# Adjacency masks as packed bytes, written by GpSimd and turned four at a time as float32

## The chip, the core and the metric

The kernel runs on one core of a Trainium2 chip. TensorE multiplies and transposes into PSUM, VectorE, ScalarE and GpSimd compute element by element (GpSimd on SBUF alone), and the queue of SyncE (SP) issues all the DMA transfers. The metric is the device time of one execution in microseconds; smaller is better.

## The reference

Two graph attention layers over 8192 nodes with 128 features and one adjacency matrix of 8192 x 8192 int32 (about 0.4% ones). Each layer normalises x, takes the ReLU, multiplies by W, and sums over the neighbours:

```
h  = relu(layernorm(x));  Wh = h @ W
e  = leaky_relu((Wh @ a_src)[:, None] + (Wh @ a_dst)[None, :], 0.2)
att = softmax(where(adj > 0, e, very negative), axis=1)
layer 0: att = where(att >= 1e-4, att, 0) * (number of neighbours)
         x = x + elu(Wh + att @ Wh)
layer 1: x = x + att @ Wh
```

The number of neighbours counts adj > 0 in each row. Layer 0 leaves out small weights, and layer 1 doesn't.

## The kernel before

A short preparation makes h, its row and column terms and their exponentials for each layer. Then a path follows that the data choose; with this input it is the fast one, `fast_path_0` for layer 0 and `fast_path_1` for layer 1. The weight of edge (i, j) is written as max(r_i, rho_j) times the mask times D_j, where D_j is multiplied into h once (`fold`, eight parts). So no exponential is taken per edge.

Layer 0 works on 16 groups of four row tiles (512 rows), with a loop over the groups 2 to 13 (`groups_of`). Each group passes over the columns in four chunks of 2048, that is 16 column tiles a chunk and 64 a group. The work per chunk:

- SP loads four pieces of int32, one for each row tile k, into `adj_in[k]` (L861). There are four such buffers in all. A piece for the next chunk is loaded when its mask has been made (semaphore `masked`).
- VectorE makes a bf16 mask of each piece (`mark`, L995) in `edges`, two buffers of four tiles.
- ScalarE sums each mask along its rows for the number of neighbours (`count`, L908).
- TensorE turns the masks: for a pair of column tiles eight bf16 transposes (L951) into one of four PSUM banks (`RING`).
- VectorE forms the weights of one column tile for 512 rows from that bank (`form`, L1002): max of `r_row` and `rho_col`, times the mask, into float32 `wTs`.
- ScalarE copies the bank as bytes into `edge_out` (L919), and SP stores a chunk of it to `edgesT` (L884), which layer 1 reads in place of the adjacency matrix.
- TensorE multiplies the weights by h, one float32 product for each row tile (L968); each is two instructions. All 64 column tiles add up in PSUM.

The order on TensorE is: turn pair p + 2, sum pair p. On VectorE: form a pair, and in the first four of each chunk's eight pairs one mask of the next chunk behind it. On ScalarE: copy a pair, and in the same places count. After pair 5 and pair 11 of a group VectorE finishes the group before (`finish`, `finish_elu`), with an ELU by ScalarE between. Before the store of the finished rows SP waits for it (`out_ready`), with the next chunk's loads behind it in its queue.

Layer 1 has eight groups of eight row tiles. Its two loads a chunk bring the masks of two groups of layer 0, 1 MB each, in pieces of 8192 bytes a partition (L1128); VectorE forms 1024 weights at a time (L1178), and TensorE makes eight products (L1162). GpSimd does nothing but three constants at the start.

Of the kernel before, what the change touches and what calls it, by code (L numbers as in the profile page):

```python
# [13 lines left out]
ALU = mybir.AluOpType  # L14
# [4 lines left out]
U8 = mybir.dt.uint8  # L19
I32 = mybir.dt.int32  # L20
# [32 lines left out]
PAIRS = T // 2  # L53
RING = 4
CP = PAIRS // NC
# [9 lines left out]
def kernel_program(nc, x, adj, W0, a0, W1, a1, out):  # L65
# [15 lines left out]
    with ctx:  # L81
# [90 lines left out]
        def prepare(layer, x_in, W_in, a_in):  # L172
# [68 lines left out]
            with nc.Block() as block:  # L241
                @block.sync
                def _(sp):
# [211 lines left out]
        def general_path(layer, x_in, x_to):  # L455
# [305 lines left out]
            return sync_rows, scalar_rows, tensor_rows, vector_rows  # L761

# [31 lines left out]
        def load_r(sp, r_loaded, i):  # L794

            c = slice(0, G0 * P) if i == 0 else slice(G0 * P, G1 * P) if i == 1 else slice(G1 * P, N)
            sp.dma_start(r_row[:, c], r_mid[:, c].partition_broadcast(P)).then_inc(r_loaded[i], 16)  # L797
# [10 lines left out]
        def fast_path_0(x_in, x_to):  # L808
# [22 lines left out]
            edges = [part(at + i * GI * CB // 2, GI * CB // 2).bitcast(BF16).rearrange("p (t c) -> p t c", t=G0)  # L831
                     for i in range(2)]
            at += GI * CB
            wTs = [part(at + i * 2 * GI, 2 * GI) for i in range(RING)]
            at += RING * 2 * GI
            edge_out = [part(at + i * CB * GI // 4, CB * GI // 4).bitcast(U8) for i in range(2)]
            at += CB * GI // 2
# [9 lines left out]
            edge_ps = [bank(i).bitcast(BF16) for i in range(RING)]  # L847

            x_view = x_in.rearrange("(g t p) f -> g p t f", p=P, t=G0)
            h_view = h_mid.rearrange("(g t p) f -> g p t f", p=P, t=G0)  # L850
            out_view = x_to.rearrange("(g t p) f -> g p t f", p=P, t=G0)

            def sync_rows(sp):
                def group(it, g):
                    for c in range(NC):
                        for k in range(G0):
# [4 lines left out]
                            sp.dma_start(adj_in[k], adj_view[it * (2 * G0) + (g * G0 + k), :, c, :])\  # L861
# [7 lines left out]
                        if c == 2:  # L869
                            if g >= 1:  # L870
                                wait_in(sp, out_ready, it, 1, g)
                                sp.dma_start(out_view[it * 2 + (g - 1)], xo.rearrange("p (t f) -> p t f", t=G0))\
                                    .then_inc(stored, 16)
                            sp.dma_start(xr.rearrange("p (t f) -> p t f", t=G0), x_view[it * 2 + g])\
                                .then_inc(res_loaded, 16)
                            sp.dma_start(hr.rearrange("p (t f) -> p t f", t=G0), h_view[it * 2 + g])\
                                .then_inc(res_loaded, 16)

                def store_edges(it, g, c):
                    if c < 0:  # L880
                        g, c = g - 1, c + NC

                    wait_in(sp, copied, it, PAIRS, g * PAIRS + (c + 1) * CP)
                    sp.dma_start(edgesT[it * (2 * NC) + (g * NC + c)], edge_out[c % 2]).then_inc(edges_stored[c % 2], 16)  # L884
# [6 lines left out]
                sp.dma_start(out_view[NG - 1], xo.rearrange("p (t f) -> p t f", t=G0)).then_inc(stored, 16)  # L891
                sp.wait_ge(stored, 16 * NG)
                for i in range(2):
                    sp.wait_ge(edges_stored[i], 16 * NG * NC // 2)

            def scalar_rows(act):
                def count(it, g, c, k):
# [10 lines left out]
                    nc.scalar.activation(copies, edges[c % 2][:, k, :], ACT.Identity,  # L908
                                         accum_out=cnt[g % 2][:, k, c:c + 1]).then_inc(counted, 1)

                def group(it, g):
                    for p in range(PAIRS):
                        c, q = p // CP, p % CP
                        m = g * PAIRS + p

                        wait_in(act, formed, it, 2 * PAIRS, 2 * (m + 1))
                        if q == 0 and g * NC + c >= 2:
                            act.wait_ge(edges_stored[c % 2], it * (NC * 16) + (g * NC + c) // 2 * 16)
                        nc.scalar.activation(edge_out[c % 2][:, q * 2 * GI:(q + 1) * 2 * GI], edge_ps[m % RING],  # L919
                                             ACT.Identity).then_inc(copied, 1)  # L920
# [17 lines left out]
            def tensor_rows(pe):  # L938
                def turn_pair(it, g, p):
                    if p >= PAIRS:  # L940
# [352 lines left out]
```

## Time and profile before

| | |
|---|---|
| Runs | 2295.46, 2295.52, 2297.7 us, median 2295.52 |
| Profiled execution, its span | 2295.8 us |
| Layer 0's path, layer 1's path in it | 1196.0 us, 928.6 us |
| TensorE, VectorE, ScalarE busy | 2161.5, 1843.8, 1047.8 us |
| Granted TensorE clock, mean | 0.978 of full speed |
| DMA | 448.32 MB, mean 195 GB/s |

The page was taken in one execution whose span, 2295.8 us, is its own time. The busy time of an engine is the time in which at least one of its instructions is under way. The mean duration of a matmul is longer than its pace, since matmuls overlap; the pace is busy time over count, or the distance of starts in the timeline.

### The profile page before, as it was taken

The page shows a single profiled execution, that of the slowest core. Times are in us where ns is not written, and L with a number is a line of the kernel's source. Part 1 is how long each engine was busy: PE and PEld are TensorE (multiplying, and loading weights), DVE is VectorE, ACT ScalarE, POOL GpSimd, SP SyncE. Part 2 cuts the span into 40 slices and gives each one's busy share as a digit, 9 for nine tenths or more (in the row PEclk, how much of TensorE's full clock was granted, in tenths as well). Part 3 has the DMA queues.
Part 4 walks back from the last instruction along what each step waited for, and adds up shares of the span by engine and source line. Part 5 has one row for each costly group of instructions (what it writes and reads, how often), then busy time and mean ns, then how long its engine had stood idle before and what let it go on. Part 6 is the DMA issues. An engine that isn't in the chain of part 4 may idle for free. (4 is left out here: it accounts for less than half of the span.)

```text
span 2295.8 us, 51629 instructions
## 1 busy us (share of the span) xinstructions
PE 2161.5 (94%) x20884; PEld 2145.0 (93%) x20884; DVE 1843.8 (80%) x2708; ACT 1047.8 (46%) x1206; POOL 1.0 (0%) x7
## 2 busy tenths in 40 slices
PE   5899999999999999999999369999999999999997
PEld 4799999999999999999999269999999999999997
DVE  6898888888888989888987657877777777777775
ACT  4788888888888878888887220000000000000000
POOL 0000000000000000000000000000000000000000
PEclk9899999999999999999999689999999999999999
DMA  6869776877777767876684332121212121212120
GB/s 221 353 264 356 293 274 237 347 303 272 269 312 304 295 249 304 330 281 268 277 350 150 92 150 83 73 93 74 93 74 92 75 92 74 92 74 92 74 93 11
DMA packets 112240, 448.32 MB, mean 195 GB/s; under 512 B 8320, under 2 KB 57984, under 8 KB 62592
## 3 DMA queue, kind: packets, MB, share of 16 engines
q1 hardware_dynamic: 112000, 444.89, 50.7%
q8 instruction: 179, 2.93, 0.5%
q14 instruction: 61, 0.50, 0.1%
HBM read 365.04 MB, written 79.82 MB: 194 GB/s over the span
## 5 line engine op out<-in xcount | busy, mean ns | idle before, releaser
L968 PE MATMUL psum<-h_all,arena 128*128 128x129 f32 x8192 | 1030.7, 279 | 1.2 <-DVE arena L1002 1.0
L968 PEld LDWEIGHTS psum<-h_all,arena 128*128 128x128 f32 x8192 | 959.0, 192 | 3.9 <-DVE arena L1002 2.3
L1162 PE MATMUL psum<-h_all,arena 128*128 128x129 f32 x8192 | 920.4, 276 | 23.6 <-DVE arena L1178 20.2
L1162 PEld LDWEIGHTS psum<-h_all,arena 128*128 128x128 f32 x8192 | 918.9, 192 | 25.2 <-issue 17.6
L1178 DVE SCALAR_TENSOR_TENSOR arena<-arena,rho_col 128x1024 f32<-128x1024 f32 (+1 forms) x512 | 653.8, 1284 | 234.8 <-PE psum L1162 225.6
L1002 DVE SCALAR_TENSOR_TENSOR arena<-arena,rho_col,psum 128x512 f32<-128x512 bf16 (+1 forms) x1024 | 710.5, 744 | 99.5 <-PE psum L951 94.8
L919 ACT ACTIVATE arena<-psum 128x1024 uint8<-128x1024 bf16 x512 | 510.5, 1021 | 154.8 <-DVE arena L1002 154.5
L908 ACT ACTIVATE arena<-arena 128x2048 bf16<-128x2048 bf16 x256 | 487.9, 1906 | 50.5 <-DVE arena L995 44.8
L995 DVE TENSOR_SCALAR arena<-arena 128x2048 bf16<-128x2048 int32 x256 | 313.1, 1224 | 38.1 <-DMA arena<-in_adj_dram 36.8
L951 PE MATMUL psum<-identb,arena 128*128 128x128 bf16 x4096 | 314.4, 220 | 22.4 <-DVE arena L995 9.8
L951 PEld LDWEIGHTS psum<-identb,arena 128*128 128x128 bf16 x4096 | 273.7, 99 | 29.9 <-DVE arena L995 9.9
L416 PE MATMUL psum<-ident,arena 128*128 128x128 f32 x128 | 23.5, 315 | 40.7 <-DVE arena L308 40.7
L416 PEld LDWEIGHTS psum<-ident,arena 128*128 128x128 f32 x128 | 17.8, 164 | 42.4 <-DVE arena L308 41.7
L908 ACT ACTIVATION_READ_ACCUMULATOR arena<-arena 128x1 f32 x256 | 49.2, 192 | 0.0
L424 PE MATMUL psum<-arena 128*128 128x131 f32 x256 | 39.1, 302 | 0.0
L424 PEld LDWEIGHTS psum<-arena 128*128 128x128 f32 x256 | 35.9, 215 | 0.6 <-ACT arena L396 0.4
L308 DVE TENSOR_SCALAR arena<-arena 128x128 f32<-128x128 f32 x128 | 33.5, 344 | 0.3
L284 DVE BATCH_NORM_STATS2 arena<-arena 128x6 f32<-128x128 f32 x128 | 25.5, 281 | 7.2 <-DMA arena<-in_x_dram 3.8
L396 ACT ACTIVATE arena<-psum 128x512 f32<-128x512 f32 x32 | 19.3, 602 | 17.0 <-PE psum L416 17.0
L385 ACT ACTIVATE h_all<-psum 128x512 f32<-128x512 f32 x32 | 19.1, 598 | 9.5 <-PE psum L424 7.8
L805 DVE TENSOR_TENSOR h_all<-h_all,D_col 128x1024 f32<-128x1024 f32 x16 | 19.5, 1221 | 0.0
L1032 DVE SCALAR_TENSOR_TENSOR arena<-psum,arena 128x128 f32<-128x128 f32 x64 | 18.0, 345 | 0.7 <-DVE arena L1028 0.2
(100 smaller groups left out, 178.3 us busy)
## 6 DMA issues: line engine op xcount, KB each, us to landing
arena<-in_adj_dram SPq DMA_DIRECT2D x256, 1024.0 KB, 8.3
edgesT<-arena SPq DMA_DIRECT2D x64, 1024.0 KB, 5.9
arena<-edgesT SPq DMA_DIRECT2D x64, 1024.0 KB, 6.6
arena<-r_mid SPq DMA_DIRECT2D x2, 3584.0 KB, 20.4
h_mid<-h_all SPq DMA_DIRECT2D x16, 256.0 KB, 2.3
arena<-in_x_dram SPq DMA_DIRECT2D x16, 256.0 KB, 3.1
arena<-h_mid SPq DMA_DIRECT2D x16, 256.0 KB, 3.5
x_mid<-arena SPq DMA_DIRECT2D x16, 256.0 KB, 2.5
```

The source lines that it names most:

```text
L284: last = nc.vector.bn_stats(st[:, t, :], x_all[:, t, :])
L308: last = nc.vector.tensor_scalar(hn[:, t, :], x_all[:, t, :], mean[:, t:t + 1], rstd[:, t:t + 1], ALU.subtract, ALU.mult)
L416: last = nc.tensor.transpose(hn_ps[q % 2][:, i * P:(i + 1) * P], hn[:, q * QT + i, :], ident[:])
L424: last = nc.tensor.matmul(h_ps[q % 2][:, i, :], hnT[q % 2][:, i * P:(i + 1) * P], W_ext, start=True, stop=True)
L908: nc.scalar.activation(copies, edges[c % 2][:, k, :], ACT.Identity, accum_out=cnt[g % 2][:, k, c:c + 1]).then_inc(counted, 1)
L919: nc.scalar.activation(edge_out[c % 2][:, q * 2 * GI:(q + 1) * 2 * GI], edge_ps[m % RING], ACT.Identity).then_inc(copied, 1)
L951: last = nc.tensor.transpose(edge_ps[m % RING][:, (b * G0 + k) * P:(b * G0 + k + 1) * P], edges[c % 2][:, k, (2 * q + b) * P:(2 * q + b + ...
L968: last = nc.tensor.matmul(acc_tile(g, G0, k), wTs[m % RING][:, b * GI + k * P:b * GI + (k + 1) * P], h_all[:, j, :], start=(j == 0 and k % ...
L995: nc.vector.tensor_scalar(edges[c % 2][:, k, :], adj_in[k], 0.0, None, ALU.is_gt).then_inc(masked, 1)
L1002: nc.vector.scalar_tensor_tensor(wTs[m % RING][:, b * GI:(b + 1) * GI], r_row[:, bass.ds(it * (2 * GI) + g * GI, GI)], rho_col[:, 2 * p + ...
L1162: last = nc.tensor.matmul(acc_tile(g, G1, k), wTs[m % RING][:, k * P:(k + 1) * P], h_all[:, j, :], start=(j == 0 and k % 2 == 0), stop=(j ...
L1178: nc.vector.scalar_tensor_tensor(wTs[m % RING].rearrange("p (h i) -> p h i", h=2), r_row[:, bass.ds(it * (2 * R1) + g * R1, R1)] .rearrang ...
```

## The change

Mask and turning, in layer 0. The masks of the four row tiles of a group are written as bytes into one buffer, `packs`, byte k of each float32 word for row tile k. GpSimd writes them (`pool_rows`), as min(adj, 1) and max with 0, with a step of four bytes. TensorE turns the words as float32, one transpose for four masks, in quads of four column tiles: a quad fills one bank. VectorE forms from every fourth byte of the bank. `wTs` has eight buffers of one column tile instead of four of two. ScalarE copies the bank as 1024 16-bit words, a quad at a time, and counts from the bytes. The order on TensorE is: turn quad q + 1, sum the four tiles of quad q.

Rows. Layer 1 wants its eight row tiles as bytes of words as well, so a group of layer 0 now takes every second row tile of eight: 0, 2, 4, 6 and then 1, 3, 5, 7. Loads, stores and `r_row` are addressed accordingly, and the first chunk's four loads, which the preparation issues, take these tiles too (`adj_view[2 * k, ...]`). In layer 1 the edge loads go into pieces of 512 bytes, and `form` reads its bytes with a step of four. The first part of `r_row` is 1024 wide in both layers, and its second part is loaded a little later in layer 1.

```diff
 RING = 4
-CP = PAIRS // NC
+WRING = 8
+QUAD = 4
+QUADS = T // QUAD
+CQ = QUADS // NC
...
-                            sp.dma_start(adj_in[k], adj_view[k, :, 0, :]).then_inc(adj_in_loaded[k], 16)
+                            sp.dma_start(adj_in[k], adj_view[2 * k, :, 0, :]).then_inc(adj_in_loaded[k], 16)
...
+            packs = [part(at + i * CH, CH) for i in range(2)]
+            pack_bytes = [p.bitcast(U8).rearrange("p (n k) -> p n k", k=G0) for p in packs]
...
+            edge_bytes = [bank(i).bitcast(U8).rearrange("p (b i k) -> p b k i", b=QUAD, k=G0) for i in range(RING)]
+            edge_words = [bank(i).bitcast(U16) for i in range(RING)]
...
+            rows_view = adj.rearrange("(a k h p) (c n) -> a h k p c n", k=G0, h=2, p=P, n=CH)
...
-                            sp.dma_start(adj_in[k], adj_view[it * (2 * G0) + (g * G0 + k), :, c, :])\
+                            sp.dma_start(adj_in[k], rows_view[it + g // 2, g % 2, k, :, c, :])\
...
+            def pool_rows(pool):
+                def group(it, g):
+                    for c in range(NC):
+                        u = g * NC + c
+                        for k in range(G0):
+                            pool.wait_ge(adj_in_loaded[k], it * (2 * NC * 16) + (u + 1) * 16)
+                            if k == 0:
+                                wait_in(pool, turned, it, QUADS, (u - 1) * CQ)
+                            wait_in(pool, counted, it, NC * G0, (u - 2) * G0 + k + 1)
+                            nc.gpsimd.tensor_scalar(pack_bytes[c % 2][:, :, k], adj_in[k], 1.0, 0.0,
+                                                    ALU.min, ALU.max).then_inc(masked, 1)
...
-                    for p in range(PAIRS):
-                        c, q = p // CP, p % CP
-                        m = g * PAIRS + p
-
-                        wait_in(act, formed, it, 2 * PAIRS, 2 * (m + 1))
+                    for q in range(QUADS):
+                        c, r = q // CQ, q % CQ
+                        m = g * QUADS + q
+
+                        wait_in(act, formed, it, T, QUAD * (m + 1))
...
-                        if q < G0:
-                            count(it, g, c + 1, q)
-                        if p == 9 and g >= 1:
+                        count(it, g, c + 1, r)
+                        if q == 4 and g >= 1:
...
-                    wait_in(pe, copied, it, PAIRS, m - RING + 1)
-                    for b in range(2):
-                        for k in range(G0):
-                            last = nc.tensor.transpose(edge_ps[m % RING][:, (b * G0 + k) * P:(b * G0 + k + 1) * P],
-                                                       edges[c % 2][:, k, (2 * q + b) * P:(2 * q + b + 1) * P],
-                                                       identb[:])
+                    wait_in(pe, copied, it, QUADS, m - RING + 1)
+                    for b in range(QUAD):
+                        last = nc.tensor.transpose(edge_ps[m % RING][:, b * P:(b + 1) * P],
+                                                   packs[c % 2][:, (QUAD * r + b) * P:(QUAD * r + b + 1) * P], ident[:])
...
-                    nc.vector.tensor_scalar(edges[c % 2][:, k, :], adj_in[k], 0.0, None, ALU.is_gt).then_inc(masked, 1)
...
+                def form(it, g, j):
+                    m = g * T + j
+                    if j % QUAD == 0:
+                        wait_in(dve, turned, it, QUADS, m // QUAD + 1)
+                    wait_in(dve, summed, it, T, m - WRING + 1)
+                    r_four = r_row[:, bass.ds(it * (2 * GI) + g // 2 * (2 * GI), 2 * GI)]\
+                        .rearrange("p (k h i) -> p k h i", k=G0, h=2)[:, :, g % 2, :]
+                    nc.vector.scalar_tensor_tensor(wTs[m % WRING].rearrange("p (k i) -> p k i", k=G0), r_four,
+                                                   rho_col[:, j:j + 1], edge_bytes[m // QUAD % RING][:, j % QUAD],
+                                                   ALU.max, ALU.mult).then_inc(formed, 1)
...
-                        if p == 5 and g >= 1:
+                        if j == 9 and g >= 1:
                             finish(it, g - 1)
-                        if p == 11 and g >= 1:
+                        if j == 22 and g >= 1:
                             finish_elu(it, g - 1)
...
-                            sp.dma_start(edges[c % 2][:, h].rearrange("p b i -> p (b i)"),
-                                         edgesT[it * (4 * NC) + ((2 * g + h) * NC + c)]).then_inc(edges_loaded[c % 2], 16)
+                            sp.dma_start(edges[c % 2][:, :, h, :],
+                                         edgesT[it * (4 * NC) + ((2 * g + h) * NC + c)]
+                                         .rearrange("p (b w) -> p b w", b=CB)).then_inc(edges_loaded[c % 2], 16)
```

On TensorE at the start of layer 0, before (L951 turns with `identb`, L968 sums):

```order
L1234 COMPARE_AND_BRANCH
L951 MATMUL psum<-identb,arena 128x128 x24
L968 MATMUL psum<-h_all,arena 128x129 x8
L951 MATMUL psum<-identb,arena 128x128 x8
L968 MATMUL psum<-h_all,arena 128x129 x8
```

and after (L970 turns with `ident`, L984 sums):

```order
L1237 COMPARE_AND_BRANCH
L970 MATMUL psum<-ident,arena 128x128 x8
L984 MATMUL psum<-h_all,arena 128x129 x16
L970 MATMUL psum<-ident,arena 128x128 x4
L984 MATMUL psum<-h_all,arena 128x129 x16
```

Eight transposes for every eight products have become four for every sixteen.

On VectorE, where group 1 finishes group 0, before (L1002 forms, L995 makes a mask, L1017 to L1032 finish):

```order
L995 TENSOR_SCALAR arena<-arena 128x2048
L1002 SCALAR_TENSOR_TENSOR arena<-arena,rho_col,psum 128x512 x4
L1017 TENSOR_REDUCE arena<-arena 128x4
L1019 COPY arena<-psum 128x1 x4
L1022 TENSOR_SCALAR arena<-r_col,low_exp 128x4
L1024 SCALAR_TENSOR_TENSOR at_risk<-arena 128x4
L1025 TENSOR_SCALAR arena<-arena 128x4
L1026 RECIPROCAL arena<-arena 128x4
L1028 TENSOR_TENSOR arena<-arena 128x4
L1032 SCALAR_TENSOR_TENSOR arena<-psum,arena 128x128 x4
L1002 SCALAR_TENSOR_TENSOR arena<-arena,rho_col,psum 128x512 x6
L995 TENSOR_SCALAR arena<-arena 128x2048
```

and after (L1006 forms, L1019 to L1034 finish, L1041 to L1045 are the second part):

```order
L1006 SCALAR_TENSOR_TENSOR arena<-arena,rho_col,psum 128x512 x25
L1019 TENSOR_REDUCE arena<-arena 128x4
L1021 COPY arena<-psum 128x1 x4
L1024 TENSOR_SCALAR arena<-r_col,low_exp 128x4
L1026 SCALAR_TENSOR_TENSOR at_risk<-arena 128x4
L1027 TENSOR_SCALAR arena<-arena 128x4
L1028 RECIPROCAL arena<-arena 128x4
L1030 TENSOR_TENSOR arena<-arena 128x4
L1034 SCALAR_TENSOR_TENSOR arena<-psum,arena 128x128 x4
L1006 SCALAR_TENSOR_TENSOR arena<-arena,rho_col,psum 128x512 x13
L1041 TENSOR_SCALAR arena<-arena 128x512
L1042 SCALAR_TENSOR_TENSOR arena<-arena 128x512
```

The masks are gone from VectorE, and the finishing stands nearly where it stood: after 10 and 23 column tiles of the next group instead of 12 and 24.

On GpSimd, which had no row in layer 0, there is now the branch and one row:

```order
L1236 TENSOR_LOAD path
L1236 ISA x2
L1237 COMPARE_AND_BRANCH
L911 ISA
L911 TENSOR_SCALAR arena<-arena 128x2048 x256
```

All 256 masks stand behind one another, each with its waits for the loaded piece, for the turning of the chunk two before, and for its count.

## Rows read from the trace of the kernel before

**Rows 1.** Page: the span, and each engine's busy time, share and instructions.

```profile
span 2295.8 us, 51629 instructions
...
PE 2161.5 (94%) x20884; PEld 2145.0 (93%) x20884; DVE 1843.8 (80%) x2708; ACT 1047.8 (46%) x1206; POOL 1.0 (0%) x7
```

**Rows 2.** Page: the chain that ended last, shares of the span by line.

```profile
PE psum L1162 38%; DVE arena L1201 1%; DVE arena L1178 1%; DVE arena L1208 1%; DMA arena<-edgesT 0%; DVE arena L1192 0%; DVE arena L1196 0%; DVE arena L1195 0%; DVE arena L1194 0%; SPq L797 0%; SPq L1233 0%; SPq L1128 0%; DVEq L1245 0%; DVEq L776 0%; DVEq L1197 0%
```

**Rows 3.** Windows of both layers' paths: busy us (instructions), clock, DMA share, GB/s.

```profile
68.00:1264.00 1196.00, 1181.91 (x12288) 1171.74 (x12288) 1046.31 (x1540) 993.10 (x1052) 0.00 (x0) 0.99 0.75 292
1351.40:2280.00 928.60, 918.64 (x8178) 917.33 (x8179) 697.15 (x707) 0.00 (x0) 0.00 (x0) 1.00 0.23 82
```

**Rows 4.** Waits: engine and line, what it waited for, us in total, times, longest.

```profile
DVE arena L1002 <- PE psum L951: 94.8, 131, 2.1
...
DVE arena L995 <- DMA arena<-in_adj_dram: 36.8, 25, 2.7
```

**Rows 5.** Page, groups: count, busy us, mean ns, idle before and its releaser.

```profile
L1162 PE MATMUL psum<-h_all,arena 128*128 128x129 f32 x8192 | 920.4, 276 | 23.6 <-DVE arena L1178 20.2
...
L1178 DVE SCALAR_TENSOR_TENSOR arena<-arena,rho_col 128x1024 f32<-128x1024 f32 (+1 forms) x512 | 653.8, 1284 | 234.8 <-PE psum L1162 225.6
L1002 DVE SCALAR_TENSOR_TENSOR arena<-arena,rho_col,psum 128x512 f32<-128x512 bf16 (+1 forms) x1024 | 710.5, 744 | 99.5 <-PE psum L951 94.8
L919 ACT ACTIVATE arena<-psum 128x1024 uint8<-128x1024 bf16 x512 | 510.5, 1021 | 154.8 <-DVE arena L1002 154.5
L908 ACT ACTIVATE arena<-arena 128x2048 bf16<-128x2048 bf16 x256 | 487.9, 1906 | 50.5 <-DVE arena L995 44.8
L995 DVE TENSOR_SCALAR arena<-arena 128x2048 bf16<-128x2048 int32 x256 | 313.1, 1224 | 38.1 <-DMA arena<-in_adj_dram 36.8
```

**Rows 6.** Timeline of layer 0, settled: start us, us, engine, line, operation.

```profile
501.52 0.61 PE L951 MATMUL psum<-identb,arena 128*128 128x128 bf16 x8
...
501.97 2.00 PE L968 MATMUL psum<-h_all,arena 128*128 128x129 f32 x16
...
503.81 0.61 PE L951 MATMUL psum<-identb,arena 128*128 128x128 bf16 x8
```

**Rows 7.** Timeline of the preparation of layer 1, TensorE.

```profile
1310.03 0.60 PE L416 MATMUL psum<-ident,arena 128*128 128x128 f32 x4
...
1310.47 1.06 PE L424 MATMUL psum<-arena 128*128 128x131 f32 x8
```

**Rows 8.** Timeline of GpSimd, all that it does before the change.

```profile
0.25 0.10 POOL L1280 MEMSET const-float32-0.0<- 128x1 f32 x1 [0.25 <-issue]
...
0.74 0.20 POOL L159 MEMSET ident<- 128x128 f32 x1 [0.29 <-POOLq L1280]
...
1.53 0.29 POOL L164 CAST identb<-ident 128x128 bf16<-128x128 f32 x1
```

**Rows 9.** Timeline of layer 0's first instructions.

```profile
62.10 0.23 DVE L803 COPY h_all<-D_col 128x64 f32<-128x64 f32 x1 [3.27 <-issue]
...
68.03 2.74 PE L951 MATMUL psum<-identb,arena 128*128 128x128 bf16 x24 [9.76 <-DVE arena L995]
```

**Rows 10.** Timeline of layer 0's last row group being finished by VectorE.

```profile
1263.86 0.17 DVE L1017 TENSOR_REDUCE arena<-arena 128x4 f32<-128x16 f32 x1 [4.01 <-PE psum L968]
...
1265.34 1.13 DVE L1032 SCALAR_TENSOR_TENSOR arena<-psum,arena 128x128 f32<-128x128 f32 x4
...
1267.82 0.43 DVE L1039 TENSOR_SCALAR arena<-arena 128x512 f32<-128x512 f32 x1 [1.36 <-ACT arena L931]
...
1269.01 0.69 DVE L1043 TENSOR_TENSOR arena<-arena 128x512 f32<-128x512 f32 x1
```

**Rows 11.** Page, DMA issues: line, count, KB each, median us to landing.

```profile
arena<-in_adj_dram SPq DMA_DIRECT2D x256, 1024.0 KB, 8.3
```

**Rows 12.** Windows: loads in pieces of 512 bytes, then loads in long pieces.

```profile
1282.00:1298.00 16.00, 1.06 (x3) 0.68 (x3) 9.55 (x53) 0.43 (x2) 0.00 (x0) 0.50 0.94 259
1344.00:1352.00 8.00, 0.57 (x3) 0.61 (x4) 2.01 (x2) 0.00 (x0) 0.00 (x0) 0.50 1.01 425
```

More of the change, by code:

```diff
@@ L19 @@
 U8 = mybir.dt.uint8
+U16 = mybir.dt.uint16
 I32 = mybir.dt.int32
@@ L829, in fast_path_0 @@
             at = 2 * N
[L831 to L837, printed above, removed]
+            packs = [part(at + i * CH, CH) for i in range(2)]
+            pack_bytes = [p.bitcast(U8).rearrange("p (n k) -> p n k", k=G0) for p in packs]
+            at += 2 * CH
+            wTs = [part(at + i * GI, GI) for i in range(WRING)]
+            at += WRING * GI
+            edge_out = [part(at + i * CB * P, CB * P).bitcast(U16) for i in range(2)]
+            at += 2 * CB * P
             copies = part(at, CH // 2).bitcast(BF16)
@@ L894, in sync_rows, with pool_rows @@
                     sp.wait_ge(edges_stored[i], 16 * NG * NC // 2)
+            def pool_rows(pool):
+                def group(it, g):
[8 more added lines that the diff above has]
+                                                    ALU.min, ALU.max).then_inc(masked, 1)
+                for g in range(NG):
+                    group(0, g)
             def scalar_rows(act):
@@ L959, in sum_pair @@
                         wait_in(pe, acc_read, it, 1, g - 1)
-                    for b in range(2):
-                        j = 2 * p + b
-                        if g == 0 and j % (T // FOLDS) == 0:
-                            pe.wait_ge(h_folded, j // (T // FOLDS) + 1)
-                        wait_in(pe, formed, it, 2 * PAIRS, m * 2 + b + 1)
-                        for k in range(G0):
-                            last = nc.tensor.matmul(acc_tile(g, G0, k),
-                                                    wTs[m % RING][:, b * GI + k * P:b * GI + (k + 1) * P],
-                                                    h_all[:, j, :], start=(j == 0 and k % 2 == 0), stop=(j == T - 1),
-                                                    skip_group_check=True)
+                    if g == 0 and j % (T // FOLDS) == 0:
+                        pe.wait_ge(h_folded, j // (T // FOLDS) + 1)
@@ L972, in sum_pair @@
+                    wait_in(pe, formed, it, T, m + 1)
+                    for k in range(G0):
+                        last = nc.tensor.matmul(acc_tile(g, G0, k), wTs[m % WRING][:, k * P:(k + 1) * P],
+                                                h_all[:, j, :], start=(j == 0 and k % 2 == 0), stop=(j == T - 1),
+                                                skip_group_check=True)
                     last.then_inc(summed, 1)
                 def group(it, g):
-                    for p in range(PAIRS):
-                        turn_pair(it, g, p + 2)
-                        sum_pair(it, g, p)
```

123 lines of the change are left out of this document (57 added, 66 removed).

## The prediction

> **What bounds the kernel now.** I read the page's first part, then the chain, then a table of stretches, then the waits, and last the timeline of a settled stretch. TensorE is busy 94% of the span and VectorE 80%, while GpSimd does nothing [rows 1]. The chain that ended last is TensorE's products of layer 1 and ends there after 38% of the span [rows 2]; it does not reach back into layer 0, so the table of stretches has to say what binds there. It gives layer 0's path 1196.0 us (68.0 to 1264.0) and layer 1's 928.6 us. In the first, TensorE is busy 1181.9 us at a granted clock of 0.99, VectorE 1046.3 us (87%), ScalarE 993.1 us (83%); in the second TensorE is busy 918.6 of 928.6 us [rows 3]. VectorE's two largest waits in layer 0 are for turned tiles, 94.8 us, and for the adjacency loads, 36.8 us [rows 4]. So TensorE binds both paths, and VectorE is close behind it in the first.
>
> The settled timeline gives TensorE's cycle: the eight bf16 transposes of a pair start at 501.52, its eight float32 products (16 instructions) at 501.97, the next transposes at 503.81 [rows 6]. That is 0.45 us of turning and 1.84 us of summing, 2.29 us for a pair of column tiles, and 512 pairs make 1172 us. The other 24 us of the 1196 are cold or uneven stretches at the start and losses between.
>
> **TensorE's work after the change.** The products stay: 16 for each four column tiles. The 16 bf16 transposes of these four tiles become 4 float32 ones, because one float32 element holds four mask bytes. The price of a float32 transpose stands in the preparation: four of them start at 1310.03 and the next product at 1310.47 [rows 7], 0.11 us each, 0.44 us for four. A product costs 920.4 / 4096 = 0.225 us in layer 1, where nothing interrupts them [rows 5], and 1.84 / 8 = 0.230 us between transposes [rows 6]. The change from turning to summing thus costs about 0.04 us each time, and the longer runs pay it half as often: 16 x 0.225 + 0.04 = 3.64 us. A quad of column tiles then costs 3.64 + 0.44 = 4.08 us where two pairs cost 4.58. 256 quads save 256 x 0.50 = 128 us. With products at 0.230 it is 118 us, with 0.225 and no change-over cost 138 us.
>
> **VectorE.** It loses the 256 masks, 313.1 us [rows 5]. It keeps 1024 forming instructions, now reading one byte of each 4-byte word of PSUM and a row vector in four pieces. No row shows a byte read from PSUM. From below the price is today's 710.5 / 1024 = 0.69 us [rows 5], since 512 elements are still 512 elements. The row of layer 1 with two operands from SBUF, one of them bytes, has 1024 elements in 1.284 us, 1.25 ns each or 0.64 us for 512, so byte operands cost nothing visible there. From above I take one such instruction of twice the elements, 1.28 us. I choose 0.70: the words touched are those that a float32 read would touch. Four formings are then 2.8 us beside TensorE's 4.08, and VectorE is hidden with 1.2 us to spare per quad. At 1.28 us it would be 5.1 us and the new bound. Layer 1's forming reads its bytes with the same step; it takes 1.28 us beside 8 x 0.225 = 1.80 us of TensorE, and it would have to become 0.5 us slower to matter. I cost it at nothing.
>
> **ScalarE.** 256 copies instead of 512 (1.02 us each [rows 5], the same 1024 elements) and the same 256 counts (1.91 us). Per quad 2.9 us and a short accumulator read beside 4.08, hidden; the copy's relief of 255 us is worth nothing in time. The count now stands behind a GpSimd mask, and behind the count stands the next copy, and TensorE turns into a bank only when the copy of four quads earlier is done. A late mask stops the whole ring by that way.
>
> **GpSimd, the open cost.** 256 masks of 2048 int32 elements to bytes four apart. It needs one mask per quad, so it stays hidden up to 4.08 us and costs nothing in the balance up to 4.58 us, today's time of two pairs. The trace has no such instruction. Its nearest rows are a memset of one element, 0.10 us, a memset of 128, 0.20 us, and a cast of 128, 0.29 us [rows 8]. With 0.10 us fixed, the cast costs 1.5 ns an element and a mask 3.1 us; the memset's slope gives 1.7 us; the cast without any fixed part gives 16 x 0.29 = 4.6 us. I take 3.1 us, because a fixed part is plainly there and a mask reads and writes as the cast does. Beyond these ends the row doesn't exclude more, since the input is an integer and there are two operations.
>
> The Trainium skill (GPSIMD Engine Reference, section 3.1) gives 1.03 cycles an element at 1.2 GHz for a body of up to two operations and about 1.8 for a tight loop otherwise; as an estimate that makes 1.8 to 3.1 us a mask, on the same side of 4.08. No run here shows that yet.
>
> **Start.** VectorE's first instruction in layer 0 is at 62.10 and TensorE's first transpose at 68.03 [rows 9], after four masks of 1.22 us. Now four masks by GpSimd stand there: 62.1 + 4 x 3.1 + 0.1 = 74.6, 6.6 us later, say 7. Masks of 1.7 us would make it 1 us, of 4.6 us 13 us. Against that, part of the 24 us of losses came from VectorE, which formed and masked at once; I give back 4 of them, with 0 and 15 as the ends.
>
> **Loads and queues.** SP keeps its order. The four adjacency buffers are refilled after each mask, each load lands 8.3 us after its issue [rows 11], and a chunk lasts 4 x 4.08 = 16.3 us; a buffer freed after its own 3.1 us is full again at 11.4 us. Traffic in layer 0 rises from 292 GB/s to 292 x 1196 / 1075 = 325, at a DMA share of 0.75 x 1.11 = 0.83 [rows 3], while 425 GB/s at full share is seen with long pieces [rows 12]. SP still stops in every group before the output store, and the four loads behind it come in one burst; GpSimd's buffers absorb that, as each chunk is masked about one chunk ahead of its turning. Layer 1's edge loads now land in pieces of 512 bytes. Loads of that kind moved 259 GB/s against 425 [rows 12]. In the settled part 2 MB are wanted per 29 us, so it is hidden. At the start 2 MB stand in front of the first forming: 8.1 us instead of 4.9 at most, of which I count 2 us, as issue and latency overlap.
>
> **VectorE against GpSimd.** VectorE finishes a row group in 1263.86 to 1266.47, 2.6 us, and again in 1.9 us [rows 10]. These instructions stand at the third and the sixth quad of the next group. TensorE has 1.4 us and 2.2 us in hand there with the new ring of eight. No row shows the two engines at work together. I count 8 us for the whole path (16 groups and seven foldings of h), with 0 below; the upper end is the second rival's.
>
> The Trainium skill (SBUF — State Buffer, section "Who interferes with whom") speaks against this change: a Vector instruction with two SBUF inputs, or in a two-port mode, and a GpSimd instruction that reads SBUF exclude each other for the whole instruction. No run here shows it yet.
>
> **Sum.** 2295.8 - 128 + 7 - 4 + 8 + 2 = 2181 us. The profiled span, 2295.8, lies 0.3 us above the median of the runs, 2295.52, so nothing is converted. Forecast: 2181 us, 5% faster, with its own range 2158 to 2200.
>
> **Rivals.** First, GpSimd becomes the bound, the case that ends slower. Masks then follow one another without a gap: 62.1 + 256 T and the last chunk's 16 us; against today's end of the path at 1264 this breaks even at T = 4.6 us. At 5.5 us it costs 256 x (5.5 - 4.6) = 230 us: 2525 us, and more if TensorE's clock falls in the gaps. For it: an integer input, a strided byte output and two operations in no row. Against it: the rows reach only 4.6 us at the worst. Between 4.08 and 4.6 us it ends between 2190 and 2296.
>
> Second, the change is made but VectorE and GpSimd hold each other up. Foldings and finishes that meet a mask wait up to 3.1 us. The finish and the second part have together five or six instructions with two SBUF operands or fast copies. If two waits of 3.1 us fall in each half, 2 x 3.1 - 1.4 = 4.8 and 2 x 3.1 - 2.2 = 4.0 us stop TensorE, 8.8 us x 15 groups = 132 us: 2305. If only one wait in each half does, 2.6 us x 15 = 39 us: 2215. For it: masks fill 12.4 of 16.3 us. Against it: they begin when a chunk's last quad has been turned, so that the third quad, 12.2 us on, finds them done. The one at the sixth quad meets the last mask alone.
>
> Third, the loads can't follow. If layer 0 stays at 292 GB/s nothing is gained: 2296. With the 36.8 us of waits [rows 4] at their present size but now on the path: 2215. For it is SP's burst; against it 425 GB/s in rows 12.
>
> Fourth, byte reads from PSUM cost 1.28 us: 256 x (5.1 - 4.58) = 133 us more, 2430 us.
>
> **Chances.** The forecast 0.66; masks over 4.6 us 0.13; masks of 4.08 to 4.6 us 0.05; the two engines against each other 0.10 (of it 0.02 slower than before); the loads 0.04; byte reads 0.02. The range 2155 to 2300 leaves out the first rival's slow part, the fourth and the tail below, 0.19 together. A change of 0.2% is what a measurement of this kernel can tell from none. Faster: 0.66 + 0.04 + 0.07 + 0.02 = 0.79; within 0.2%: 0.04; slower: 0.17.
>
> **What would show it.** In the profile after, GpSimd has 256 instructions, and from start to start within a chunk they lie 3 us apart; 4.1 or more means the first rival. TensorE's transposes in layer 0 number 1024, four in 0.44 us, and quads follow at 4.08 us. VectorE's forming stays at 0.69 to 0.75 us; waits of VectorE inside the finish would speak for the second rival, GpSimd waiting for the adjacency loads with TensorE waiting for GpSimd for the third. Layer 1's products take 920 us as before. The forecast is wrong if the median is over 2200 us or if TensorE waits for masks beyond the first chunk.

## The result and the profile after

The changed kernel takes 2183.59 us (median of 3, 2180.18 to 2185.07) against 2295.52 us, a ratio of 0.9505 [0.9489, 0.9522]. The forecast was 2181 us. The sum came out; some of its terms did not, and the experiments say which.

The page of the kernel after, its first part, the chain that ended last and the groups that answer to [rows 1, 2, 5]:

```profile
span 2181.8 us, 44712 instructions
PE 2023.8 (93%) x17812; PEld 2015.4 (92%) x17812; DVE 1563.2 (72%) x2452; ACT 808.1 (37%) x950; POOL 639.2 (29%) x263
...
PE 40%; DVE 2%; DMA 1%; issue 1%; SPq 0%; DVEq 0%
...
L984 PE MATMUL psum<-h_all,arena 128*128 128x129 f32 x8192 | 969.0, 277 | 0.2 <-DVE arena L1006 0.2
...
L1162 PE MATMUL psum<-h_all,arena 128*128 128x129 f32 x8192 | 920.8, 276 | 28.2 <-DVE arena L1178 22.4
...
L1006 DVE SCALAR_TENSOR_TENSOR arena<-arena,rho_col,psum 128x512 f32<-128x512 uint8 (+1 forms) x1024 | 693.9, 742 | 274.0 <-PE psum L970 256.0
L1178 DVE SCALAR_TENSOR_TENSOR arena<-arena,rho_col 128x1024 f32<-128x1024 f32 (+1 forms) x512 | 653.7, 1284 | 239.8 <-PE psum L1162 228.4
L911 POOL TENSOR_SCALAR arena<-arena 128x2048 uint8<-128x2048 int32 x256 | 638.2, 2528 | 480.9 <-DMA arena<-in_adj_dram 282.1
...
L970 PE MATMUL psum<-ident,arena 128*128 128x128 f32 x1024 | 156.9, 277 | 42.0 <-issue 27.6
```

TensorE still binds both layers. VectorE fell from 80% to 72% and waits 256 us for turned tiles, GpSimd has one mask per quad at 2.5 us, and layer 1's two large groups are what they were. The waits of TensorE after:

```profile
PE psum L970 <- issue: 27.6, 5, 5.7
PE psum L1162 <- DVE arena L1178: 22.4, 7, 15.9
PE psum L970 <- POOL arena L911: 14.4, 1, 14.4
...
PE psum L1162 <- issue: 5.8, 1, 5.8
```

TensorE waits for a mask once, at the start, and never for a copy or a forming in the settled part. What stands out is "issue" (idle time for which the profile shows nothing that the engine waits for), five times 5.5 us, of which the prediction spoke nowhere. The settled stretch, TensorE alone (start, duration), answers to [rows 6]:

```profile
501.58 0.60 PE L970 MATMUL psum<-ident,arena 128*128 128x128 f32 x4
502.02 3.74 PE L984 MATMUL psum<-h_all,arena 128*128 128x129 f32 x32
505.60 0.60 PE L970 MATMUL psum<-ident,arena 128*128 128x128 f32 x4
506.03 3.74 PE L984 MATMUL psum<-h_all,arena 128*128 128x129 f32 x32
509.61 0.60 PE L970 MATMUL psum<-ident,arena 128*128 128x128 f32 x4
```

From transposes to transposes it is 4.01 us: 0.43 for four float32 transposes, 3.58 for 16 products. And this is the same engine where the loop over row groups jumps back, the first of five such places:

```profile
328.46 0.60 PE L970 MATMUL psum<-ident,arena 128*128 128x128 f32 x4
328.90 3.74 PE L984 MATMUL psum<-h_all,arena 128*128 128x129 f32 x32
338.24 1.11 PE L970 MATMUL psum<-ident,arena 128*128 128x128 f32 x4 [5.61 <-issue]
339.14 5.77 PE L984 MATMUL psum<-h_all,arena 128*128 128x129 f32 x32
344.75 0.60 PE L970 MATMUL psum<-ident,arena 128*128 128x128 f32 x4
```

The engine stands still for 5.6 us with nothing in the profile that it waits for, and the next quad takes 6.5 us instead of 4.01, with transposes at 1.11 us instead of 0.60: from 338 to 344 us the granted clock is 0.55, near the lower of its two levels (1.2 of 2.4 GHz), after it was 1.00 until the stop. This jump costs 9.78 + 6.51 - 2 x 4.01 = 8.3 us, the other four 8.0 to 8.1 us each, and the five 40.5 us. In the trace of before the same five jumps have gaps of 2.4 to 2.7 us, three of them with a slower pair behind, 18.0 us together. They are hard to see there, since the wait rows put three of them down to ScalarE's copy:

```profile
PE psum L951 <- ACT arena L919: 7.8, 3, 2.7
PE psum L951 <- issue: 4.9, 2, 2.4
```

The 114.0 us between the two spans divide as follows. The quads' pace: 256 x (4.58 - 4.01) = 146 us less. Stops and slow stretches in layer 0, which is all that the quads' pace leaves over: 44.8 us instead of 23.3, 21.5 more; at the five jumps alone 40.5 instead of 18.0. TensorE's start in layer 0: 72.39 instead of 68.03, 4.4 more. Between the layers: 90.9 instead of 87.6 us, 3.3 more, since VectorE's first forming of layer 1 waits 11.4 us for the edge loads instead of 9.2. Layer 1: 2.8 more, mostly its own one jump (5.8 us after, 3.5 before).

### The profile page after: what moved, and what is told of

It is laid out like the page before. It is cut to its first block and busy times, and to the rows that moved or that the text cites. A ratio compares the mean times of both kernels' runs of the same rounds, so it can differ in the third digit from the quotient of the medians.

```text
span 2181.8 us, 44712 instructions
## 1 busy us (share of the span) xinstructions
PE 2023.8 (93%) x17812; PEld 2015.4 (92%) x17812; DVE 1563.2 (72%) x2452; ACT 808.1 (37%) x950; POOL 639.2 (29%) x263
## 5 line engine op out<-in xcount | busy, mean ns | idle before, releaser
L984 PE MATMUL psum<-h_all,arena 128*128 128x129 f32 x8192 | 969.0, 277 | 0.2 <-DVE arena L1006 0.2
L984 PEld LDWEIGHTS psum<-h_all,arena 128*128 128x128 f32 x8192 | 947.1, 194 | 1.1 <-issue 0.5
L1162 PE MATMUL psum<-h_all,arena 128*128 128x129 f32 x8192 | 920.8, 276 | 28.2 <-DVE arena L1178 22.4
L1006 DVE SCALAR_TENSOR_TENSOR arena<-arena,rho_col,psum 128x512 f32<-128x512 uint8 (+1 forms) x1024 | 693.9, 742 | 274.0 <-PE psum L970 256.0
L911 POOL TENSOR_SCALAR arena<-arena 128x2048 uint8<-128x2048 int32 x256 | 638.2, 2528 | 480.9 <-DMA arena<-in_adj_dram 282.1
L929 ACT ACTIVATE arena<-arena 128x2048 bf16<-128x2048 uint8 x256 | 487.9, 1906 | 37.8 <-POOL arena L911 37.8
L940 ACT ACTIVATE arena<-psum 128x1024 uint16<-128x1024 uint16 x256 | 261.4, 1021 | 287.1 <-DVE arena L1006 286.4
L970 PE MATMUL psum<-ident,arena 128*128 128x128 f32 x1024 | 156.9, 277 | 42.0 <-issue 27.6
L970 PEld LDWEIGHTS psum<-ident,arena 128*128 128x128 f32 x1024 | 122.4, 143 | 43.2 <-issue 28.5
L419 PE MATMUL psum<-ident,arena 128*128 128x128 f32 x128 | 24.0, 320 | 41.4 <-DVE arena L311 41.4
L419 PEld LDWEIGHTS psum<-ident,arena 128*128 128x128 f32 x128 | 18.3, 167 | 43.1 <-DVE arena L311 42.4
L287 DVE BATCH_NORM_STATS2 arena<-arena 128x6 f32<-128x128 f32 x128 | 25.5, 277 | 6.9 <-DMA arena<-in_x_dram 3.6
L801 DVE TENSOR_TENSOR h_all<-h_all,D_col 128x1024 f32<-128x1024 f32 x16 | 26.4, 1651 | 0.0
L1041 DVE TENSOR_SCALAR arena<-arena 128x512 f32<-128x512 f32 x16 | 6.8, 427 | 21.9 <-ACT arena L951 21.9
```

What stands on the lines that cost most here:

```text
L419: last = nc.tensor.transpose(hn_ps[q % 2][:, i * P:(i + 1) * P], hn[:, q * QT + i, :], ident[:])
L801: nc.vector.tensor_tensor(h_all[:, c, 0:F], h_all[:, c, 0:F], D[:, c].to_broadcast([P, T // FOLDS, F]), ALU.mult).then_inc(h_folded, 1)
L911: nc.gpsimd.tensor_scalar(pack_bytes[c % 2][:, :, k], adj_in[k], 1.0, 0.0, ALU.min, ALU.max).then_inc(masked, 1)
L929: nc.scalar.activation(copies, pack_bytes[c % 2][:, :, k], ACT.Identity, accum_out=cnt[g % 2][:, k, c:c + 1]).then_inc(counted, 1)
L940: nc.scalar.activation(edge_out[c % 2][:, r * 2 * GI:(r + 1) * 2 * GI], edge_words[m % RING], ACT.Identity).then_inc(copied, 1)
L970: last = nc.tensor.transpose(edge_ps[m % RING][:, b * P:(b + 1) * P], packs[c % 2][:, (QUAD * r + b) * P:(QUAD * r + b + 1) * P], ident[:])
```

## The experiments

**1. TensorE's loop of layer 0 written out.** In the changed kernel:

```
-                groups_of(pe, NG, group)
+                for g in range(NG):
+                    group(0, g)
```

> The changed kernel with TensorE's loop over the groups of layer 0 written out (no jump back; every other engine keeps its loop). Theory A (TensorE waits for its own instructions after each of the five jumps, behind the bulk loads in the DMA engines): the gaps of 5.4 to 5.7 us and the slow quad behind each go, 8.3 us x 5 = 41 us, so 2183.6 - 41 = about 2142 us. Rival B (TensorE stands there because data or other engines are late): the gaps stay, 2179 to 2188 us.

Measured: 2142.08 us, 0.9328 [0.9313, 0.9344] of before, 41.5 us less than the change alone. The stops and the slow quads behind them are gone; from 72.4 to 1090 us TensorE is busy 1017.43 of 1017.6 us. Theory A holds to the microsecond.

**2. The same edit in the kernel before.**

> The kernel before, with TensorE's loop over row groups of layer 0 written out (no jump), the other engines as they are. Theory A (TensorE's own stop at the jump of its loop costs time in both kernels, 23.3 us over five jumps before and 44.8 after): 2295.8 - 20 = 2276 us, 2270 to 2282; written out, the change is then worth 2276 - 2142 = 134 us instead of 112. Theory B (before, TensorE's stops at the jump are covered by VectorE, which is late there anyway): no difference, 2296 us.

Measured: 2281.53 us, 0.9942 [0.9925, 0.9958], 14 us less. Theory A, at the small end. The gaps put down to ScalarE's copy are gone as well, so they too belonged to the jump. The expectation's 23.3 us were not all at the jumps: these had cost 18.0 us, and TensorE's part of layer 0 is 16.0 us shorter in the profile (1179.8 instead of 1195.8 us). So with TensorE's jumps of layer 0 gone on both sides the change is worth 2281.5 - 2142.1 = 139.4 us; 28 of these (41.5 - 14.0) were given away at five jumps.

**3. Every quad's transposes twice.** `for b in [*range(QUAD), *range(QUAD)]` in place of `for b in range(QUAD)`.

> The changed kernel, with the four float32 transposes of each quad issued twice (same data, same place). Theory A (TensorE binds layer 0, and a transpose costs its pace of 0.11 us in full): 256 x 0.44 = 113 us more, 2184 + 113 = 2296 us, 2288 to 2300. Theory B (part of a quad's 4.01 us is waiting for VectorE, ScalarE or GpSimd): clearly less, under 2270 us.

Measured: 2292.14 us, 0.9986 [0.9977, 0.9996], 108.5 us more or 0.424 us for four transposes, which is their pace in the timeline. Nothing in a quad's 4.01 us was waiting that could have hidden them: TensorE alone sets the pace of layer 0.

**4. Why the stop is long: lighter loads.**

```
+                            w = CH if g < 2 else CH // 4
-                            sp.dma_start(adj_in[k], rows_view[..., c, :])
+                            sp.dma_start(adj_in[k][:, :w], rows_view[..., c, :w])
```

> The changed kernel, but from the third row group of layer 0 on each adjacency load brings only the first quarter of its columns (this leaves out three quarters of the input; instructions, waits and loops are the same). Theory A (TensorE's stop at its loop jump is 5.4 to 5.7 us instead of 2.5 because the load traffic is full there, share 0.99): the stops go back to 2.7 us or less and the slow quad behind them goes, 5 x (8.3 - 4) = 20 us less, 2164 us, 2155 to 2170. Theory B (the longer stop belongs to the loop itself, whatever the loads do): the stops stay at 5.4 us and the time at 2184 us, 2178 to 2186.

Measured: 2173.74 us, 0.9472 [0.9456, 0.9488] of before, 10 us less than the change, between the two. The first jump there, TensorE alone:

```profile
329.31 3.74 PE L985 MATMUL psum<-h_all,arena 128*128 128x129 f32 x32
336.99 0.75 PE L971 MATMUL psum<-ident,arena 128*128 128x128 f32 x4 [3.94 <-issue]
337.53 5.32 PE L985 MATMUL psum<-h_all,arena 128*128 128x129 f32 x32
342.69 0.60 PE L971 MATMUL psum<-ident,arena 128*128 128x128 f32 x4
```

With the DMA share around the jump (326 to 346 us) down from 0.89 to 0.32 the stop is 3.9 us, not 2.7, and a slow quad still follows. So the light loads take 1.5 us off each stop, and with what hangs on it 2 us of the 8.1. That is no test without traffic, though. Inside the first stop itself the engines were still busy; the kernel before, the kernel after and the light loads (from and to, length, busy us of each engine, clock, DMA share, GB/s):

```profile
366.43:368.86 2.43, 0.00 (x1) 0.00 (x1) 2.02 (x3) 2.43 (x3) 0.00 (x0) 0.99 0.68 206
332.63:338.24 5.61, 0.01 (x2) 0.01 (x1) 1.74 (x3) 2.91 (x3) 3.92 (x2) 0.85 1.00 402
333.05:336.99 3.94, 0.00 (x1) 0.01 (x1) 0.00 (x0) 2.44 (x3) 2.33 (x1) 1.00 0.75 247
```

The traces show one thing more. In each stop a 16 KB transfer of the kind "instruction" starts on queue q8, and TensorE goes on 1.5 to 1.7 us after its start in all 40 jump stops of layer 0 in eight traces (before, after, and experiments 3 to 7). What differs is when it starts: within 0.2 us of the stop's beginning in the kernel before, 1.3 to 1.7 us later with the light loads, 2.9 to 3.1 us later in the changed kernel. So the whole difference between the stops lies ahead of that transfer. At TensorE's waits for masks in experiment 7 no such transfer stands at that distance. The profile does not say which engine it is for; that TensorE waits for it is read from this agreement, not tested.

**5. The other engines' jumps taken away.** SP, ScalarE and VectorE written out in layer 0, TensorE's loop left; then the same with the light loads.

> The changed kernel with the loops of SP, ScalarE and VectorE in layer 0 written out, and TensorE's left as a loop. Theory A (TensorE's stop is long because the other engines fetch their own loop bodies at the same time): its stops fall from 5.4 us to about 2.5 us and the quad behind them is less slow, 5 x 3 to 4 us, 2166 us, 2163 to 2170. Theory B (the stop is TensorE's own, whatever the others do): 2184 us, 2180 to 2186.

> The same with the light loads (from the third row group on each adjacency load brings only the first quarter of its columns, which leaves out three quarters of the input). With TensorE's loop alone and little traffic. Light loads by themselves gave 2174 us and stops of 4.0 us. Theory A (traffic and the other engines' fetches each add their part): stops of 2.5 us or less, 2160 us, 2155 to 2166. Theory B (only traffic adds): 2174 us, 2171 to 2176, stops of 4.0 us.

Measured: 2181.22 us, 0.9494 [0.9478, 0.9510], stops of 26.6 us in sum; and 2173.53 us, 0.9467 [0.9448, 0.9485], stops of 21.7 us. Theory B in both: the other engines' jumps cost TensorE nothing that can be told from noise. The stop belongs to TensorE's own jump, and lighter loads shorten it. Why 4.0 to 4.3 us remain with them, where it is 2.5 us before, stays open; since they left a share of 0.75 inside the stop, traffic may still be a part of it.

**6. GpSimd's masks in the kernel before.** The bf16 masks moved from VectorE to GpSimd, with everything else as before.

> The kernel before with its bf16 masks made by GpSimd (min with 1, max with 0) in place of VectorE, all else as before: the move to GpSimd alone. Theory A (TensorE binds with 2.29 us a pair, VectorE's relief is worth only the uneven stretches at the start): start 4 us later, 4 to 8 us won back, 2288 to 2300 us. Rival B (VectorE's 87% was what slowed layer 0): 60 us and more go, under 2240 us.

Measured: 2312.98 us, 1.0076 [1.0060, 1.0093], 13 us above theory A's range and far from rival B. The pair of column tiles still takes 2.29 us. Relieving VectorE by itself gains nothing and costs 17 us; the gain of the change is TensorE's cheaper turning. What theory A had not counted are the jumps: with the slower pairs behind them they cost 35.3 us instead of 18.0. Waits of TensorE and the group of masks there:

```profile
PE psum L966 <- issue: 26.5, 5, 5.5
...
PE psum L966 <- POOL arena L908: 12.3, 1, 12.3
```

```profile
L908 POOL TENSOR_SCALAR arena<-arena 128x2048 bf16<-128x2048 int32 x256 | 485.0, 1911 | 764.5 <-issue 446.9 <-DMA arena<-in_adj_dram 317.5
```

The longer stop is here too, with bf16 masks and bf16 transposes. So the packing is not needed for it. Nor is the move: the kernel of experiment 7, with packed masks by VectorE and GpSimd idle, has five such stops too, of 5.0 to 5.9 us. What the three kernels share is full load traffic inside the stop, a DMA share of 0.94 to 1.00 where it is 0.62 to 0.72 before; that this makes the stop long fits experiment 4 but was not tested by itself.

**7. The opposite: packed masks by VectorE.** GpSimd idle, a mask behind each quad's formings.

```
+                        if j % QUAD == QUAD - 1:
+                            mark(it, g, j // CB + 1, j // QUAD % G0)
```

> The changed kernel with the packed byte masks made by VectorE, one behind each quad of formings, and GpSimd idle: the packed turning alone. Theory A (a byte mask written with a step of four bytes costs VectorE the 1.22 us of the bf16 mask): VectorE has 1024 x 0.68 + 313 + 26 + 60 = about 1096 us of work in layer 0 where TensorE has 1071, so VectorE binds by a little: 2205 to 2240 us. Rival B (the strided byte output halves its rate, 2.3 us): 2.72 + 2.3 = 5.0 us per quad, 256 x 5.0 + 86 = 1370 us, so about 2480 us.

Measured: 2353.54 us, 1.0250 [1.0233, 1.0267]. Neither number. A mask took 1.38 us and four formings 2.72, in all 4.10 us where TensorE wants 4.01, and the chunk's last mask comes last. TensorE's wait rows and one such place, VectorE above, TensorE below:

```profile
PE psum L958 <- DVE arena L997: 126.3, 64, 10.0
...
PE psum L958 <- issue: 27.6, 5, 5.9
```

```profile
510.28 1.37 DVE L997 TENSOR_SCALAR arena<-arena 128x2048 uint8<-128x2048 int32 x1
```

```profile
506.57 0.60 PE L958 MATMUL psum<-ident,arena 128*128 128x128 f32 x4
507.00 3.74 PE L972 MATMUL psum<-h_all,arena 128*128 128x129 f32 x32
511.78 0.65 PE L958 MATMUL psum<-ident,arena 128*128 128x128 f32 x4 [1.04 <-DVE arena L997]
```

One wait per chunk, 64 in all: 126 of the 170 us between this kernel and the changed one; the rest I did not divide. With float32 transposes VectorE cannot carry the masks in this order, so the move to GpSimd is what lets the packing pay: packed turning with VectorE's masks is 58 us slower than before, GpSimd's masks with the old turning 17 us slower, both together 112 us faster.

**8. Each GpSimd mask made twice.**

> The changed kernel with each mask made twice by GpSimd, so that a mask costs 2 x 2.4 = 4.8 us and more. Theory A (above TensorE's 4.01 us per quad GpSimd sets the pace, as the first rival of the prediction priced it): layer 0's path ends near 61.7 + 256 x 4.8 + 16 = 1307 instead of 1143.7, so 2183.6 + 163 = about 2347 us, and more by what the wait between the two costs. Rival B (the two mask buffers and the idle time of GpSimd in each chunk hide most of it): under 2230 us.

Measured: 2549.79 us, 1.1106 [1.1084, 1.1128] (two runs), 200 us above the larger forecast. GpSimd's cycle is 4.97 us for two masks (500.36, 505.30, 510.28), as expected. But VectorE's finishing chain of a row group, 2.6 us long before [rows 10], now meets masks without a gap. First VectorE in the kernel after, then in this one, at the same instructions:

```profile
483.97 0.29 DVE L1024 TENSOR_SCALAR arena<-r_col,low_exp 128x4 f32 x1 [0.17 <-DVE arena L1021]
484.42 0.16 DVE L1026 SCALAR_TENSOR_TENSOR at_risk<-arena 128x4 f32 x1 [0.16 <-DVE arena L1024]
...
485.01 0.17 DVE L1030 TENSOR_TENSOR arena<-arena 128x4 f32<-128x4 f32 x1
```

```profile
537.84 2.58 DVE L1029 TENSOR_SCALAR arena<-r_col,low_exp 128x4 f32 x1 [0.15 <-DVE arena L1026]
540.56 2.20 DVE L1031 SCALAR_TENSOR_TENSOR at_risk<-arena 128x4 f32 x1
...
543.17 2.12 DVE L1035 TENSOR_TENSOR arena<-arena 128x4 f32<-128x4 f32 x1
```

Three instructions on four elements take 2.1 to 2.6 us each, about a mask's length, and the finish lasts 9.2 us. TensorE's transposes of two quads lie 11.63 us apart there instead of 4.01, 5.63 us of it idle. Its two largest waits in the whole run:

```profile
PE psum L975 <- POOL arena L916: 153.8, 34, 24.5
PE psum L989 <- DVE arena L1011: 116.1, 28, 6.1
```

The second row, 28 waits for a forming, is the prediction's second rival: up to 6.1 us each and 116 us in all, where it had priced 4.8 and 4.0 us, 132 us in all. In the changed kernel it did not occur: the masks of that chunk begin at 486.09, just before the finish ends (486.74).

**9. The exclusion measured by itself.** 100 more masks by GpSimd on unused memory beside layer 1.

> The changed kernel, with 100 more masks by GpSimd of the same shape, on memory that nothing else uses, beside layer 1, where VectorE forms with two operands from SBUF (1.28 us each, one wanted per 1.79 us of TensorE). Theory A (a GpSimd mask and such a VectorE instruction exclude each other for their whole length): a mask and a forming take 2.4 + 1.28 = 3.7 us in turn where TensorE wants one forming per 1.8 us, so each mask costs up to 1.9 us: 2184 + 190 = 2374 us, 2320 to 2380. Theory B (they share the memory without waiting): VectorE's forming stays at 1.28 us and the time at 2184 us, 2180 to 2190.

Measured: 2346.68 us, 1.0216 [1.0199, 1.0233], 163 us more. VectorE, then GpSimd (five formings in 16.88 us, twelve masks in 40.21 us):

```profile
1248.16 16.88 DVE L1178 SCALAR_TENSOR_TENSOR arena<-arena,rho_col 128x1024 f32<-128x1024 f32 x5
1264.97 3.44 DVE L801 TENSOR_TENSOR h_all<-h_all,D_col 128x1024 f32<-128x1024 f32 x1
```

```profile
1247.30 40.21 POOL L1234 TENSOR_SCALAR arena<-arena 128x2048 uint8<-128x2048 int32 x12
```

Both engines advance one instruction per 3.36 us, in turn, where alone they take 1.28 and 2.40. 95 of the masks lie beside layer 1, and 96 formings took 335 us, 3.49 us each, where TensorE's pace asks for one per 1.79 us: 96 x (3.49 - 1.79) = 163 us. Theory A, nearly the whole of both lengths (3.36 of 3.68).

**10. TensorE's loops written out in both layers.**

> The changed kernel with TensorE's loops over row groups written out in both layers. Layer 1 has one jump left, with a stop of 5.8 us. Theory A (each stop is lost in full): 2142 - 6 = 2136 us, 2133 to 2139. Theory B (the stop of layer 1 is partly won back by the ring of formed tiles, or more code brings stops of its own): 2139 us or more.

Measured: 2134.11 us, 0.9294 [0.9279, 0.9310]. Theory A. This is the fastest kernel of the study, 49.5 us faster than the change and 161 us faster than before.

**11. The first chunk's masks shared.** On top of it VectorE makes columns 0 to 1279 of the first four masks.

> The changed kernel with TensorE's loops written out in both layers (2134 us), and the masks of the first chunk shared: VectorE makes columns 0 to 1279 of each of the four, GpSimd columns 1280 to 2047. Theory A (the two exclude each other, 4 x (0.86 + 0.9) = 7.0 us instead of 9.8 us, then VectorE's foldings): TensorE's first transpose 2.5 to 3.5 us earlier, 2131 us, 2129 to 2132. Theory B (they run side by side): 6 us earlier, 2128 us. Theory C (the start is covered by something else, such as VectorE's foldings or the loads of the second chunk, which now go out later): 2134 us or more.

Measured: 2135.8 us, 0.9298 [0.9283, 0.9314]: theory C. The start of layer 0 there, GpSimd, VectorE, TensorE, and TensorE's later waits:

```profile
60.09 5.90 POOL L916 TENSOR_SCALAR arena<-arena 128x768 uint8<-128x768 int32 x4 [58.25 <-issue]
60.12 6.59 DVE L1070 TENSOR_SCALAR arena<-arena 128x1280 uint8<-128x1280 int32 x4 [3.27 <-issue]
...
66.77 1.97 PE L976 MATMUL psum<-ident,arena 128*128 128x128 f32 x8 [10.36 <-DVE arena L1070]
...
83.66 0.66 PE L976 MATMUL psum<-ident,arena 128*128 128x128 f32 x4 [1.21 <-POOL arena L916]
```

TensorE's first transpose comes 5.8 us earlier (66.77 against 72.54). The lead is lost by the third chunk: TensorE waits for masks at 83.66 and at 102.72, and its tenth quad starts at 108.43 against 108.09. GpSimd waits for loads (5.60 us before its first full mask), which in this kernel could only start when the shared masks were done. The last transposes of the layer stand at 1095.55 against 1095.95. By these waits the start is here bound by the loads of the next chunks; a start with early masks and early loads was not tried.

## Why the prediction was right, step by step

- *TensorE binds before and after, and the gain is its turning.* Right: experiments 3 and 6.
- *A quad of 4.08 us.* It is 4.01. The price of a float32 transpose, read in the preparation [rows 7], was right to 0.01 us. The wrong piece is the 0.04 us for the change from turning to summing: 16 x 0.224 + 0.43 = 4.01 leaves nothing for it with float32 transposes. Of the 0.57 us saved, 0.47 are transposes (0.90 - 0.43) and 0.10 products (3.68 - 3.58). The term was -128 and is -146, beyond even the bound of 138.
- *"The other 24 us of the 1196 are cold or uneven stretches at the start and losses between"*, of which 4 were to come back. This is the step that failed. Most of those losses, 18.0 of 23.3 us, sat at TensorE's five loop jumps. The losses did not shrink but grew to 44.8 us, +21.5 instead of -4. A look at the five gaps of 2.4 to 2.7 us in the trace of before would have shown the place, though not that it would grow; the wait rows hide it, with two marked "issue" and three put down to ScalarE's copy.
- *Start +7.* It is +4.4: the four masks take 10.7 us instead of 12.4, 2.40 us each but for one that took 3.4 us beside VectorE's copy and first folding, and they begin at 61.65 instead of 62.10. Whether the 4.4 us are on the path for good is not shown: experiment 11 started 5.8 us earlier and gained nothing, but its loads went out later too.
- *VectorE's forming 0.70 us.* 693.9 / 1024 = 0.68, and 0.66 from start to start. Byte reads from PSUM four apart cost no more than before; the fourth rival is dead.
- *A GpSimd mask of 3.1 us.* It is 2.40 us from start to start, inside the bounds 1.7 and 4.6 and nearer the lower. The first rival, over 4.08, was out of reach. The estimate of 1.8 to 3.1 us that the prediction worked out from the Trainium skill (GPSIMD Engine Reference, section 3.1) holds the measured 2.40 us. Experiment 8 shows the bound that it would have been: with 4.97 us per quad the layer is bound by GpSimd, and dearer than the formula 256 T says, because the second rival's mechanism comes on top.
- *VectorE against GpSimd +8.* In the changed kernel it is about 0 in the settled part, since finishes and masks miss each other, as the prediction's "against it" said. At the start it shows in VectorE, where it is nearly hidden: a COPY of 64 elements takes 2.48 us (0.23 before), and three foldings 3.0 to 3.1 us instead of 1.22. The Trainium skill (SBUF — State Buffer, section "Who interferes with whom") says that such instructions exclude each other for the whole instruction; experiments 8 and 9 nearly agree, with 2.1 to 2.6 us for four elements and 3.36 us for one of each in turn, a little under the 3.68 us of both lengths.
- *The loads follow.* Right: 328 GB/s at a share of 0.83 from 72.4 to 1105 us, against 325 and 0.83 forecast.
- *Layer 1 +2.* It is +6.1, of it 2.2 the wait for edge loads in 512-byte pieces, and 2.3 its jump.

So the sum of -115 us met the measured -114.0 because errors of both signs met. Dearer than forecast: 25.5 us at the stops and 4.1 us in and before layer 1. Cheaper: 18 us of the quads, 8 us of the engines' conflict, 2.6 us of the start. The mechanism of the gain was right; the agreement to 3 us is luck. Two rivals in the prediction are also slightly off as sums: 2173 + 39 is 2212, not 2215, and the same 36.8 us on 2181 give 2218.

## What to carry to other kernels

When a change shortens the bound engine's work, list its stops by place instead of carrying them over as a lump, loop jumps above all; here each grew from 3.6 to 8.1 us on average and took back 28 of 139 us. If the program has room, write out the loop of the bound engine only: here the other engines' loops cost nothing. When work moves to GpSimd, ask for gaps where VectorE's chains of small instructions can pass: with masks in 2.4 of every 4.0 us they passed here, and with GpSimd full three small instructions of the chain took about a mask's length each.

## What the runs showed that I had not expected

- A stop of 2.4 to 2.7 us at TensorE's jump before, 5.4 to 5.7 after, 5.1 to 5.5 with bf16 masks by GpSimd, 3.9 to 4.2 with light loads, 4.3 on average with light loads and the other loops written out. In the changed kernel and in experiments 4 and 5 a quad of 5.4 to 6.9 us instead of 4.01 stands behind each (granted clock 0.55 for 338 to 344 us); before, three of the five have a pair of 3.7 to 3.9 us instead of 2.29 behind them.
- An instruction transfer that starts 1.5 to 1.7 us before TensorE goes on, in all 40 jump stops looked at, whatever the stop's length.
- GpSimd's int32 mask of 2048 elements: 2.40 us into bytes four apart, about 1.9 us into contiguous bf16. VectorE: 1.38 and 1.22 us.
- VectorE and GpSimd in turn at 3.36 us, less than the 3.68 us of both lengths: a small part of each instruction does overlap.
